# Two down projections of the last weight group, each made of seven half products instead of eight

## The chip, the core and the metric

The kernel runs on one core of one Trainium2 chip. The metric is the device time of one execution in microseconds (us), as the median of several runs. The core has a matrix engine (TensorE, PE in the profile, with PEld for its weight loads), a vector engine (VectorE, DVE), an activation engine (ScalarE, ACT), a general engine (GpSimd, POOL) and an engine that issues transfers (SyncE, SP). Each works through its own list of instructions in order and waits on semaphores for the others.

## What is computed

One transformer layer on 2048 tokens of 512 features: a gated linear attention in chunks of 128 tokens, and a feed-forward part with 4-bit weights. The change lies in the feed-forward part:

```python
vals = NVFP4_LUT[idx]                                   # two 4-bit codes per byte
W = vals.reshape(N, K // 32, 32) * scales[:, :, None]   # Wg, Wu: 4096 x 512, Wd: 512 x 4096
gate = jnp.einsum('th,nh->tn', xt, Wg)                  # xt = layernorm(x), 2048 x 512
up = jnp.einsum('th,nh->tn', xt, Wu)
inter = gelu(gate) * up
out = jnp.einsum('tn,hn->th', inter, Wd)                # the down projection
x = x + out
```

## The kernel before

Every operand of a product is split in two float16 parts, high and low, and a product is made of three matmuls (high by high, high by low, low by high) that add up in one PSUM bank. The high part is a cast on ACT, the low part a subtraction on POOL (`inter_high`, `inter_low` for the intermediates; `dequant` for the weights).

The 4096 intermediates are worked through in 8 weight groups `g` of 512. A group and a block of 512 tokens make a number `n` (`n = 4g + block`, 0 to 31). `i = 4n + j` is 128 intermediates for that token block, and a pair `m` is `i = 2m` and `2m + 1` (even and odd, `e` and `o`), so pairs `2n` and `2n + 1` are what the down projection of `n` takes. The last group has `n` 28 to 31; `n` 29 and 30 are made from pairs 58 to 61.

For a pair (m from 8 on), gate and up are each made by seven half products `P1` to `P7` of six matmuls with 256 columns (`product`), after Winograd's scheme: weights and tokens are summed beforehand, and ACT and DVE combine the results (`snapshot` on ACT copies a partial sum out of the bank, `combine` on DVE adds one to it; `C11`, `C22`, `C12` are the combined parts). The banks are few, so `P7` waits for the snapshot of `P6`, and `P4` for that of `P7`. In between, PE works at the down projection of `n = m // 2 - 1`: `down` makes one tile of 128 tokens (`tt`) from four `j` with 3 matmuls of 512 columns each, six between `P6` and `P7` (called the first place in what follows) and six between `P7` and `P4` (the second place). Down projections alternate between PSUM banks 6 and 7; DVE adds a finished tile to its rows of the output `X1` (`gather`) and frees the bank.

PE's list for one pair is thus: gate P1, P5, P2, P6, first place, P7, second place, P4, P3, then the same for up. A pair's intermediates come into the tile `fw` (gelu on ACT, times up on DVE, `inter`), the last of them (the even `i`) right after the pair's last product, when PE is already in the next pair. There, ACT makes the high parts of the pair before (`inter_high`), POOL the low parts (`inter_low`), and DVE gathers a tile of the down projection.

Weights of a group come in six chunks `k = 6g` to `6g + 5`: two for gate, two for up, two for down, each with two nibbles. Where weights must be summed (gate and up), POOL makes four sums in a chain (`dq_difference`, `dq_chain`) and then their low parts (`dq_sums`), in pairs with `m % 8` of 4 or 7. There the chain comes behind `inter_low` in POOL's list. Chunks 46 and 47, the down weights of the last group, are dequantized in pairs 56 and 57.

The order of the work is written out by hand, in a loop over `m` on each engine; semaphores count each kind of step. After pair 63 follows the down projection of `n = 31` and the last stores of `X1`.

Of the kernel before, what the change touches and what calls it, by code (L numbers as in the profile page):

```python
# [5 lines left out]
F32 = mybir.dt.float32  # L6
# [65 lines left out]

DEQUANTED = (0, 1, 4, 5, 8, 9)
# [13 lines left out]
for _i in sorted(range(NI), key=nth):  # L87
    ILO[_i] = 1 + sum(on_pool(j) == on_pool(_i) for j in ILO)
# [40 lines left out]
def block_kernel(nc, x, wqkv, bqk, bv, wab, bab, codes, scales, out, cla):  # L129
    with ExitStack() as ctx:  # L130
# [93 lines left out]

        def slot(i):
# [3 lines left out]
            return ihl_r[:, j] if n >= 3 and n % 2 else ihl_s[:, j]  # L229

# [50 lines left out]
        s_prod, s_snap, s_comb = sem("s_prod"), sem("s_snap"), sem("s_comb")  # L281
        s_half, s_done = sem("s_half"), sem("s_done")
# [17 lines left out]
        def _(eng):  # L300
# [183 lines left out]
            def products(kind, m, n, tt):  # L484
# [52 lines left out]
                down(n, tt, (0, 1))  # L537
# [25 lines left out]
            def down_last(js):  # L563
# [79 lines left out]
            banks.ring = [6, 2, 3, 7]  # L643
# [11 lines left out]
        def _(eng):  # L655
# [58 lines left out]
            def gelu(i, pg, at=0):  # L714
                if i >= 2:
# [3 lines left out]
            def inter_high(i):  # L719
                n = i // 4  # L720
                ac.wait_ge(s_inter, whole(i))
                before = {1: 0, 4: 1}[n] if n in (1, 4) else (n - 2 if n > 4 else -1)
                if before >= 0:
# [869 lines left out]
```

## Time and profile before

| | |
|---|---|
| time, median of 3 runs | 1144.14 us (1143.7 to 1144.48) |
| the profiled execution: its time, its span | 1143.82 us, 1141.8 us |
| PE busy | 1136.0 us, 99% of the span |
| DVE, POOL, ACT busy | 61%, 47%, 39% |
| chain that ended last | PE 96% |
| granted TensorE clock | 1.000 |

The span is the time from the first to the last instruction; 2.0 us of the execution lie around it. An engine's busy time is the time in which at least one of its instructions ran. Matmuls overlap: the duration shown of one (273 or 379 ns) is longer than the distance from one to the next, so the pace of PE is read from the start of one run of matmuls to the start of the next, or from the chain, whose pieces don't overlap.

### The profile page before, as it was taken

The numbers are of one execution on the slowest core, as the hardware profiler recorded it, in microseconds if no ns is written. First come the engines' busy times: TensorE is split into PE (matmuls) and PEld (weight loads), VectorE is DVE, ScalarE is ACT, GpSimd is POOL, SyncE is SP. The second block draws the span as 40 slices with busy tenths as digits, with TensorE's granted clock in tenths as the row PEclk, the third lists the DMA queues.
The fourth block names the chain that finished last, engine by engine and source line by source line (L and its number), as shares of the span: only waits on it lengthen the run. The fifth ranks groups of instructions, "written<-read, shape, count | busy, mean of one in ns | idle before, by whom it ended". The sixth has DMA issues, their size and how long they took to land.

```text
span 1141.8 us, 19963 instructions
## 1 busy us (share of the span) xinstructions
PE 1136.0 (99%) x8014; PEld 787.4 (69%) x8014; DVE 694.8 (61%) x1284; ACT 446.1 (39%) x1037; POOL 535.3 (47%) x530
## 2 busy tenths in 40 slices
PE   9999999999999999999999999999999999999999
PEld 5666655565467777777777777777777777777776
DVE  7788656367777855665566556655665566555334
ACT  4433334253344434343434343434343434343332
POOL 3386535155883945363536363635362536253110
PEclk9999999999999999999999999999999999999999
DMA  8021011000101010101010101010101010100111
GB/s 303 3 76 46 29 38 38 10 10 2 56 19 38 20 37 20 38 19 38 20 37 20 38 19 38 20 38 19 38 20 37 18 38 22 34 17 16 38 38 65
DMA packets 22828, 41.97 MB, mean 37 GB/s; under 512 B 2704, under 2 KB 3024, under 8 KB 22736
## 3 DMA queue, kind: packets, MB, share of 16 engines
q1 hardware_dynamic: 22736, 40.70, 11.3%
q8 instruction: 63, 1.03, 0.4%
q14 instruction: 29, 0.24, 0.1%
HBM read 36.46 MB, written 4.23 MB: 36 GB/s over the span
## 4 chain that ended last, share of the span: by engine, by line
PE 96%; POOL 1%; DVE 1%; ACT 0%; issue 0%; DMA 0%; SPq 0%; DVEq 0%; ACTq 0%; POOLq 0%
PE ps L518 45%; PE ps L558 29%; PE ps L348 8%; PE ps L479 7%; PE ps L314 1%; PE ps L440 1%; PE ps L423 1%; PE ps L447 1%; PE ps L434 1%; PE ps L358 1%; PE ps L414 1%; DMA WR<-wqkv 0%; POOL bigA L1302 0%; DVE wf L1122 0%; POOL kn_s L1327 0%
## 5 line engine op out<-in xcount | busy, mean ns | idle before, releaser
L558 PE MATMUL ps<-WR,ihl_s 128*128 128x512 f16 x768 | 184.7, 379 | 0.0
L518 PE MATMUL ps<-XT,WR 128*128 128x256 f16 x1344 | 183.3, 273 | 0.0
L518 PE MATMUL ps<-REG,WR 128*128 128x256 f16 x1344 | 183.3, 273 | 0.0
L1139 DVE TENSOR_TENSOR load<-load,ps 128x256 f32<-128x256 f32 x168 | 70.7, 421 | 179.8 <-PE ps L518 101.3
L558 PE MATMUL ps<-WR,vv 128*128 128x512 f16 x708 | 171.4, 379 | 0.0
L518 PEld LDWEIGHTS ps<-REG,WR 128*128 128x128 f16 x1344 | 131.5, 98 | 39.1
L814 ACT COPY load<-ps 128x256 f32<-128x256 f32 x168 | 62.6, 372 | 245.1 <-PE ps L518 245.1
L1139 DVE TENSOR_TENSOR bigB<-bigB,ps 128x256 f32<-128x256 f32 x168 | 70.6, 420 | 124.3 <-ACT bigB L814 93.2
L518 PEld LDWEIGHTS ps<-XT,WR 128*128 128x128 f16 x1344 | 131.5, 98 | 15.4
L814 ACT COPY bigB<-ps 128x256 f32<-128x256 f32 x168 | 62.6, 373 | 172.0 <-PE ps L518 172.0
L558 PEld LDWEIGHTS ps<-WR,ihl_s 128*128 128x128 f16 x768 | 75.2, 98 | 66.5
L1359 POOL TENSOR_TENSOR WR<-wf,WR 128x512 f16<-128x512 f32 x40 | 48.4, 1229 | 136.6 <-ACT WR L748 136.6
L558 PEld LDWEIGHTS ps<-WR,vv 128*128 128x128 f16 x708 | 69.3, 98 | 59.2
L1343 POOL TENSOR_TENSOR vv<-fw,vv 128x512 f16<-128x512 f32 x54 | 69.4, 1308 | 66.3 <-ACT vv L729 66.3
L1343 POOL TENSOR_TENSOR ihl_s<-fw,ihl_s 128x512 f16<-128x512 f32 x56 | 72.2, 1311 | 57.4 <-ACT ihl_s L729 57.4
L1077 DVE SCALAR_TENSOR_TENSOR X<-ps,X 128x512 f32<-128x512 f32 x127 | 86.6, 682 | 17.4 <-PE ps L558 17.3
L518 PE MATMUL ps<-REG,bigA 128*128 128x256 f16 x672 | 91.7, 273 | 0.0
L348 PE MATMUL ps<-XT,WR 128*128 128x512 f16 x384 | 86.8, 379 | 0.0
L479 PE MATMUL ps<-XT,WR 128*128 128x512 f16 x384 | 85.0, 379 | 0.0
L518 PEld LDWEIGHTS ps<-REG,bigA 128*128 128x128 f16 x672 | 65.8, 98 | 19.6 <-ACT bigB L814 0.2
L1354 POOL TENSOR_TENSOR WR<-bigC,WR 128x512 f16<-128x512 f32 x28 | 34.4, 1248 | 95.2 <-ACT WR L767 95.2
L1061 DVE SCALAR_TENSOR_TENSOR fw<-fw,bigB 128x256 f32<-128x256 f32 x112 | 72.9, 650 | 3.8
(180 smaller groups left out, 1793.6 us busy)
## 6 DMA issues: line engine op xcount, KB each, us to landing
load<-codes SPq DMA_DIRECT2D x48, 256.0 KB
load<-scales SPq DMA_DIRECT2D x48, 256.0 KB
y<-X SPq DMA_DIRECT2D x15, 256.0 KB, 2.0
bigA<-cla SPq DMA_DIRECT2D x14, 256.0 KB, 3.0
X<-x SPq DMA_DIRECT2D x3, 1024.0 KB, 13.2
WR<-wqkv SPq DMA_DIRECT2D x2, 1024.0 KB, 9.6
X<-x SPq DMA_DIRECT2D x4, 256.0 KB, 3.9
WR<-wqkv SPq DMA_DIRECT2D x4, 256.0 KB, 4.3
```

The costliest lines, as they stand in the source:

```text
L314: t = eng.transpose(PS[bank][:, 128 * kt:128 * kt + 128], src, ident[:, :])
L348: mm = eng.matmul(PS[bank][:, :], lhs, rhs, start=(n == 0), stop=(n == 11))
L479: mm = eng.matmul(bank[:, :], buf[:, wp, o + kt, 128 * j:128 * j + 128], XT[:, xp, kt, 512 * b:512 * b + 512], start=(n == 0), stop=(n == 11))
L518: mm = eng.matmul(half_bank(kind, name), w(wp, kt), x(xp, kt), start=(first and n == 0), stop=(n == 5), skip_group_check=True)
L558: mm = eng.matmul(PS[bank][:, :], ih[:, ip, 128 * tt:128 * tt + 128], buf[:, wp, 8 + j, :], start=(j == 0 and p == 0), stop=(j == end and ...
L814: eng.copy(start, half_bank(kind, name)).then_inc(s_snap, 1)
L1061: eng.scalar_tensor_tensor(w, w, GS * IS, pu, ALU.mult, ALU.mult).then_inc(s_inter, 1)
L1077: eng.scalar_tensor_tensor(X1[:, T, :], PS[bank_of["dn", n, tt]][:, :], 1.0 / (WS * IS), X1[:, T, :], ALU.mult, ALU.add).then_inc(s_ev, 1)
L1139: eng.tensor_tensor(c, c, half_bank(kind, end), ALU.add).then_inc(s_comb, 1)
L1343: eng.tensor_tensor(ih[:, 1, :], fw[:, i % 2, :], ih[:, 0, :], ALU.subtract).then_inc(s_ilop, 1)
L1354: eng.tensor_tensor(buf[:, 1, base + nib, :], wf2[:, nib, :], buf[:, 0, base + nib, :], ALU.subtract).then_inc(s_wl1, 1)
L1359: eng.tensor_tensor(buf[:, 1, base + nib, :], wf[:, nib, :], buf[:, 0, base + nib, :], ALU.subtract).then_inc(s_wlo, 1)
```

## The change

The down projections of `n` 29 and 30 (`SEVEN`) are no longer made by `down`, tile after tile. Each is a product of 512 tokens by 512 intermediates by 512 columns, and is divided in two along all three, which would make eight half products; after Winograd's scheme seven are made (`seven`), of 12 matmuls with 256 columns each. They need sums of the weights (chunks 46 and 47: the chain of four sums and their low parts, POOL in pairs 57 and 58) and of the intermediates (four differences for each of the pairs 58 to 61 on DVE, `operand_sums`, in the tile `tsum`), and high and low parts of both. The parts of a pair are now three: `e` (256 columns), `o` (512) and `T` (the four sums, 1024), by `operands_high` on ACT and `operands_low` on POOL, in place of two of 512 columns each.

The seven products take the places between gate's and up's products in pairs 60 and 61 (for `n` 29) and 62 and 63 (for `n` 30): in the even pair P1, P2, P5 and P6 in the four places, in the odd pair P3, P7 and P4, the last in two halves of six matmuls. They use banks 6 and 7 and add up there; after each, DVE adds the bank to a block of `X1` (`into_rows`), and the next product in the same bank waits for that (`s_out7`). DVE has seven such steps for an `n` where it had four.

So that the halves of the weights lie right, the host gives out the 4096 intermediates in another order, for all groups, and the rows of the down weights are read in the order `at(j)`. The stores of the rows of `n` 29 and 30 wait for `P4` and `P7`.

```diff
+SEVEN = (29, 30)
+SEVEN_PAIRS = tuple(m for n in SEVEN for m in (2 * n, 2 * n + 1))
+SUMMED = 47
+IN_TURN = ("P1", "P2", "P5", "P6", "P3", "P7", "P4")
...
+def seventh(n, name):
+
+    return 7 * (n - SEVEN[0]) + IN_TURN.index(name) + 1
+
+
+def operand(m, part):
+
+    return 3 * (m - SEVEN_PAIRS[0]) + {"e": 1, "o": 2, "T": 3}[part]
...
+        tsum = load[:, 0:2, :].bitcast(F32).rearrange("p a (t n) -> p (a t) n", t=2)
+        S1 = [two(WR0[:, a, 7, :]) for a in range(2)]
...
+        def at(j):
+
+            return 8 + 2 * (j % 2) + j // 2
...
+        def part_of(m, a, part):
+
+            first, count = {"e": (0, 1), "o": (1, 2), "T": (3, 4)}[part]
+            cols = slice(256 * (m % 2), 256 * (m % 2) + 256)
+            if m // 2 == SEVEN[0]:
+                return WR0[:, a, first:first + count, cols]
+            return ihl_s[:, 0:4, a, cols] if part == "T" else WR0[:, a, 8 + first:8 + first + count, cols]
...
+                if n in SEVEN:
+                    seven_first(kind, m, n)
+                else:
+                    down(n, tt, (0, 1))
                 pe.wait_ge(s_snap, pair_base(kind, m, 3) + 2)
                 product("P7", comb(1), sums(2))
-                down(n, tt, (3, 2))
+                if n in SEVEN:
+                    seven_second(kind, m, n)
+                else:
+                    down(n, tt, (3, 2))
...
+            def seven(n, name, tts=(0, 1)):
+
+                bank = 6 if name in ("P1", "P6", "P7", "P4") else 7
+                last = {"P1": "P4", "P2": "P3", "P5": "P2", "P3": "P5", "P6": "P1", "P7": "P6", "P4": "P7"}[name]
+                if name in ("P1", "P2"):
+                    if n > SEVEN[0]:
+                        pe.wait_ge(s_out7, seventh(n - 1, last))
+                    else:
+                        for sm, value in banks.freed[bank]:
+                            pe.wait_ge(sm, value)
+                else:
+                    pe.wait_ge(s_out7, seventh(n, last))
+                pe.wait_ge(s_whi, whi_count(SUMMED, 1))
+                pe.wait_ge(s_wlo, wlo_count(SUMMED, 1))
+                pe.wait_ge(s_wsum, pair_count(SUMMED))
+                part = {"P1": "e", "P2": "o", "P3": "o"}.get(name, "T")
+                at = {"P3": 1, "P6": 1, "P7": 2, "P4": 3}.get(name, 0)
+                pe.wait_ge(s_olo, operand(2 * n + 1, part))
...
+                for tt in tts:
+                    for u in range(2):
+                        for ip, wp in ((0, 0), (0, 1), (1, 0)):
+                            x = part_of(2 * n + u, ip, part)[:, at, 128 * tt:128 * tt + 128]
+                            mm = eng.matmul(PS[bank][:, 256 * tt:256 * tt + 256], x, weight(wp, u),
+                                            start=(name in ("P1", "P2", "P5") and tt == u == ip == wp == 0),
+                                            stop=(u == 1 and ip == 1), skip_group_check=True)
+                if tts[-1]:
+                    mm.then_inc(s_seven, 1)
...
+            def seven_first(kind, m, n):
+                if m % 2 == 0:
+                    seven(n, "P1" if kind == "gate" else "P5")
+                elif kind == "gate":
+                    seven(n, "P3")
+                else:
+                    seven(n, "P4", (0,))
+
+            def seven_second(kind, m, n):
+                if m % 2 == 0:
+                    seven(n, "P2" if kind == "gate" else "P6")
+                elif kind == "gate":
+                    seven(n, "P7")
+                else:
+                    seven(n, "P4", (1,))
...
+            def operands_high(m):
+
+                ac.wait_ge(s_inter, whole(2 * m))
+                ac.wait_ge(s_prod, pair_base("up", 55, 7) + 7)
+                if m // 2 > SEVEN[0]:
+                    ac.wait_ge(s_dn, 4 * SEVEN[0])
+                eng.copy(part_of(m, 0, "e")[:, 0, :], fw[:, 0, 0:256]).then_inc(s_ohi, 1)
+                eng.copy(part_of(m, 0, "o"), two(fw[:, 1, :])).then_inc(s_ohi, 1)
+                ac.wait_ge(s_dsum, 4 * (m - SEVEN_PAIRS[0]) + 4)
+                eng.copy(part_of(m, 0, "T"), tsum).then_inc(s_ohi, 1)
...
+                if m - 1 in SEVEN_PAIRS:
+                    operands_high(m - 1)
+                elif m > 8:
                     inter_high(oo - 2)
...
+            def into_rows(n, name):
+
+                half, odd = {"P1": (0, 0), "P2": (0, 0), "P5": (1, 1), "P6": (1, 0), "P3": (1, 0), "P7": (1, 1),
+                             "P4": (0, 1)}[name]
+                bank = 6 if name in ("P1", "P6", "P7", "P4") else 7
+                block_ = X1_of(n, half, odd)
+                dv.wait_ge(s_seven, seventh(n, name))
+                earlier = {"P2": "P1", "P3": "P6", "P7": "P5"}.get(name)
+                if earlier:
+                    dv.wait_ge(s_out7, seventh(n, earlier))
+                eng.scalar_tensor_tensor(block_, PS[bank][:, :].rearrange("p (t u n) -> p t u n", t=2, u=2),
+                                         1.0 / (WS * IS), block_, ALU.mult, ALU.add).then_inc(s_out7, 1)
+
+            def operand_sums(m):
+                e, o, at = fw[:, 0, :], fw[:, 1, :], 4 * (m - SEVEN_PAIRS[0])
+                if m > SEVEN_PAIRS[0]:
+                    dv.wait_ge(s_olo, operand(m - 1, "T"))
+                dv.wait_ge(s_inter, whole(2 * m))
+                eng.tensor_tensor(tsum[:, 0, :], e[:, 256:512], e[:, 0:256], ALU.subtract).then_inc(s_dsum, 1)
+                eng.tensor_tensor(tsum[:, 2, :], o[:, 256:512], e[:, 256:512], ALU.subtract).then_inc(s_dsum, 1)
+                dv.wait_ge(s_dsum, at + 1)
+                eng.tensor_tensor(tsum[:, 1, :], o[:, 256:512], tsum[:, 0, :], ALU.subtract).then_inc(s_dsum, 1)
+                dv.wait_ge(s_dsum, at + 3)
+                eng.tensor_tensor(tsum[:, 3, :], o[:, 0:256], tsum[:, 1, :], ALU.subtract).then_inc(s_dsum, 1)
...
+            def rows_of_second(m):
+
+                n = m // 2 - 1
+                if n in SEVEN:
+                    for name in (("P5", "P6"), ("P4",))[m % 2]:
+                        into_rows(n, name)
+                else:
+                    gather(n, 2 * m % 4 + 1)
+
...
-                    inter_low(oo - 2)
-                    inter_low(ee - 2)
-                    gather((m - 1) // 2 - 1, 2 * (m - 1) % 4 + 1)
+                    rows_of_second(m - 1)
...
-                gather(n, 2 * m % 4)
+                if n in SEVEN:
+                    for name in (("P1", "P2"), ("P3", "P7"))[m % 2]:
+                        into_rows(n, name)
+                else:
+                    gather(n, 2 * m % 4)
...
+                if m in SEVEN_PAIRS:
+                    operand_sums(m)
...
+            def operands_low(m):
+                for part, src in (("e", fw[:, 0:1, 0:256]), ("o", two(fw[:, 1, :])), ("T", tsum)):
+                    pl.wait_ge(s_ohi, operand(m, part))
+                    eng.tensor_tensor(part_of(m, 1, part), src, part_of(m, 0, part), ALU.subtract).then_inc(s_olo, 1)
...
+                if m - 1 in SEVEN_PAIRS:
+                    operands_low(m - 1)
+                elif m > 8:
                     inter_low(2 * m - 1)
                     inter_low(2 * m - 2)
+                if m == 58:
+                    dq_sums(SUMMED)
...
+                if m == 57:
+                    dq_difference(SUMMED)
+                    dq_chain(SUMMED)
...
-                sp.wait_ge(s_ev, 4 * (NI // 4 - 4) + T + 1)
+                n = NI // 4 - 4 + T // 4
+                if n in SEVEN:
+                    sp.wait_ge(s_out7, seventh(n, "P7" if T % 4 >= 2 else "P4"))
+                else:
+                    sp.wait_ge(s_ev, row_done(n, T % 4))```

POOL's list from pair 56 on, before: the low parts of chunks 46 and 47 (written to `WR`), each followed by the intermediates of a pair (to `ihl_s` or `vv`).

```order
L1343 TENSOR_TENSOR vv<-fw,vv 128x512 x2
L1359 TENSOR_TENSOR WR<-wf,WR 128x512 x2
L1343 TENSOR_TENSOR ihl_s<-fw,ihl_s 128x512 x2
L1359 TENSOR_TENSOR WR<-wf,WR 128x512 x2
L1343 TENSOR_TENSOR ihl_s<-fw,ihl_s 128x512 x2
L1343 TENSOR_TENSOR vv<-fw,vv 128x512 x4
```

The same stretch of POOL's list after the change (chunk 47 comes from `bigC` now):

```order
L1508 TENSOR_TENSOR vv<-fw,vv 128x512 x2
L1529 TENSOR_TENSOR WR<-wf,WR 128x512 x2
L1508 TENSOR_TENSOR ihl_s<-fw,ihl_s 128x512 x2
L1529 TENSOR_TENSOR WR<-bigC,WR 128x512 x2
L1536 TENSOR_TENSOR bigB<-wf 128x512
L1544 TENSOR_TENSOR wf<-wf,bigC 128x4x128
L1546 TENSOR_TENSOR wf<-wf 128x4x128
L1552 TENSOR_TENSOR bigC<-bigC,wf 128x4x128
L1508 TENSOR_TENSOR ihl_s<-fw,ihl_s 128x512 x2
L1567 TENSOR_TENSOR bigA<-bigB,bigA 128x512
L1567 TENSOR_TENSOR WR<-wf,WR 128x512
L1567 TENSOR_TENSOR bigA<-wf,bigA 128x512
```

The chain of four sums (L1536 to L1552) stands between chunk 47 and the low parts of pair 57 (the `ihl_s` row behind it).

DVE's list at the turn from pair 60 to pair 61, before: the last `inter` of pair 60, the tile gathered, and the combinations of gate of pair 61.

```order
L1061 SCALAR_TENSOR_TENSOR fw<-fw,bigB 128x512
L1077 SCALAR_TENSOR_TENSOR X1<-ps7,X1 128x512
L1139 TENSOR_TENSOR load<-load,ps4 128x256
L1139 TENSOR_TENSOR load<-load,ps3 128x256 x2
L1077 SCALAR_TENSOR_TENSOR X1<-ps6,X1 128x512
```

The same place after the change:

```order
L1188 SCALAR_TENSOR_TENSOR fw<-fw,bigB 128x512
L1225 TENSOR_TENSOR load<-fw 128x256
L1226 TENSOR_TENSOR load<-fw 128x256
L1228 TENSOR_TENSOR load<-fw,load 128x256
L1230 TENSOR_TENSOR load<-fw,load 128x256
L1217 SCALAR_TENSOR_TENSOR X1<-ps7,X1 128x4x128
L1217 SCALAR_TENSOR_TENSOR X1<-ps6,X1 128x4x128
L1291 TENSOR_TENSOR load<-load,ps4 128x256
L1291 TENSOR_TENSOR load<-load,ps3 128x256 x2
L1217 SCALAR_TENSOR_TENSOR X1<-ps7,X1 128x4x128
L1217 SCALAR_TENSOR_TENSOR X1<-ps6,X1 128x4x128
```

The four differences of intermediates stand ahead of the additions to `X1` that free banks 7 and 6.

ACT's list in the first half of a pair behind one of the pairs 58 to 61, before: the snapshot of P1, the two high parts, the snapshots of P6 and P7, and two gelus.

```order
L814 COPY load<-ps 128x256
L729 CAST vv<-fw 128x512 x2
L814 COPY load<-ps 128x256 x2
L717 ACTIVATE fw<-load 128x256
L717 ACTIVATE fw<-ps 128x256
```

The same place after the change:

```order
L933 COPY load<-ps 128x256
L843 CAST WR<-fw 128x256
L844 CAST WR<-fw 128x2x256
L846 CAST WR<-load 128x4x256
L933 COPY load<-ps 128x256 x2
L821 ACTIVATE fw<-load 128x256
L821 ACTIVATE fw<-ps 128x256
```

The high part of the sums (L846) now stands ahead of the snapshot of P6.

## Rows read from the trace of the kernel before

**Rows 1.** The page: busy times; granted clock and GB/s in 40 slices.

```profile
PE 1136.0 (99%) x8014; PEld 787.4 (69%) x8014; DVE 694.8 (61%) x1284; ACT 446.1 (39%) x1037; POOL 535.3 (47%) x530
...
PEclk9999999999999999999999999999999999999999
...
GB/s 303 3 76 46 29 38 38 10 10 2 56 19 38 20 37 20 38 19 38 20 37 20 38 19 38 20 38 19 38 20 37 18 38 22 34 17 16 38 38 65
```

**Rows 2.** The chain that ended last, from 1113 us on: start, us, what.

```profile
1113.16 3.93 PE ps L518 x36
...
1128.82 3.88 PE ps L558 x18
```

**Rows 3.** Busy time of each engine in pair 63.

```profile
1114.30:1128.65 14.35, 14.35 (x110) 10.56 (x108) 5.26 (x11) 4.60 (x11) 2.27 (x2) 1.00 0.10 38
```

**Rows 4.** Timeline, PE, pair 63: gate P1, first place, P7, second place.

```profile
1114.30 0.82 PE L518 MATMUL ps<-XT,WR 128*128 128x256 f16 x6
...
1116.92 1.46 PE L558 MATMUL ps<-WR,ihl_s 128*128 128x512 f16 x6
1118.22 0.82 PE L518 MATMUL ps<-REG,bigD 128*128 128x256 f16 x6
1118.87 1.46 PE L558 MATMUL ps<-WR,ihl_s 128*128 128x512 f16 x6
```

**Rows 5.** Timeline, DVE, pair 63: the even intermediates of pair 62, and a gather.

```profile
1114.96 0.69 DVE L1061 SCALAR_TENSOR_TENSOR fw<-fw,bigB 128x512 f32<-128x512 f32 x1
1115.57 0.68 DVE L1077 SCALAR_TENSOR_TENSOR X<-ps,X 128x512 f32<-128x512 f32 x1
```

**Rows 6.** Timeline, ACT, pair 63: snapshot of P1, high parts, snapshot of P6.

```profile
1115.21 0.37 ACT L814 COPY load<-ps 128x256 f32<-128x256 f32 x1 [2.94 <-PE ps L518]
1115.48 1.14 ACT L729 CAST vv<-fw 128x512 f16<-128x512 f32 x2
1117.12 0.37 ACT L814 COPY load<-ps 128x256 f32<-128x256 f32 x1 [0.50 <-PE ps L518]
```

**Rows 7.** Timeline, POOL, pair 63: low parts.

```profile
1116.18 2.27 POOL L1343 TENSOR_TENSOR vv<-fw,vv 128x512 f16<-128x512 f32 x2 [12.08 <-ACT vv L729]
```

**Rows 8.** Timeline around the start of pair 58: POOL twice, DVE, PE's second place.

```profile
1041.12 2.44 POOL L1359 TENSOR_TENSOR WR<-wf,WR 128x512 f16<-128x512 f32 x2 [8.31 <-ACT WR L748]
1044.43 2.27 POOL L1343 TENSOR_TENSOR ihl_s<-fw,ihl_s 128x512 f16<-128x512 f32 x2 [0.87 <-ACT ihl_s L729]
...
1043.21 0.90 DVE L1061 SCALAR_TENSOR_TENSOR fw<-fw,bigB 128x512 f32<-128x512 f32 x1
...
1047.12 1.46 PE L558 MATMUL ps<-WR,ihl_s 128*128 128x512 f16 x6
```

**Rows 9.** Timeline, POOL, pair 55: first of four chained sums, first low part behind them.

```profile
1004.07 1.27 POOL L1366 TENSOR_TENSOR bigB<-wf 128x512 f32<-128x512 f32 x1
...
1009.43 1.15 POOL L1393 TENSOR_TENSOR bigA<-bigB,bigA 128x512 f16<-128x512 f32 x1
```

**Rows 10.** Timeline, DVE (chained token sums) and POOL side by side, at 313 us.

```profile
312.91 0.68 DVE L1131 TENSOR_TENSOR REG<-REG 128x512 f32<-128x512 f32 x1
313.63 1.54 DVE L1131 TENSOR_TENSOR REG<-REG 128x512 f32<-128x512 f32 x1
...
313.46 1.16 POOL L1354 TENSOR_TENSOR WR<-bigC,WR 128x512 f16<-128x512 f32 x1 [0.63 <-ACT WR L767]
314.58 1.60 POOL L1354 TENSOR_TENSOR WR<-bigC,WR 128x512 f16<-128x512 f32 x1
```

**Rows 11.** Groups by line and form: the smallest POOL subtraction, and DVE's combinations.

```profile
L1295 POOL TENSOR_TENSOR bigD<-bigD 128x64 f16<-128x64 f32 x1 | 0.3, 315 | 0.1
L1139 DVE TENSOR_TENSOR load<-load,ps 128x256 f32<-128x256 f32 x168 | 70.7, 421 | 179.8 <-PE ps L518 101.3 <-ACT load L814 76.5
```

**Rows 12.** Timeline, PE: 19 transposes at the start, and four later on.

```profile
1.75 4.14 PE L583 MATMUL ps<-bigC 128*128 128x128 f32 x19 [1.75 <-POOL bigC L1421]
...
25.40 0.60 PE L314 MATMUL ps<-bigC,bigA 128*128 128x128 f32 x4
```

More of the change, by code:

```diff
@@ L77, in nth @@
 def nth(i):
-    return i + 1 if i < 16 else (i ^ 1) + 1
+    if i < 16:
+        return i + 1
+    return (i ^ 1) + 1 - (4 * len(SEVEN) if i // 4 > SEVEN[-1] else 0)
 def on_pool(i):
@@ L86 @@
 ILO = {}
-for _i in sorted(range(NI), key=nth):
+for _i in sorted((i for i in range(NI) if i // 4 not in SEVEN), key=nth):
     ILO[_i] = 1 + sum(on_pool(j) == on_pool(_i) for j in ILO)
@@ L188, in wide @@
                 return WRX[:, g % 2, a, j]
+            if kind == "down":
+                return WRX[:, 0, a, j]
             return GX[j][a] if g % 2 else XT[:, a, 0:2, 512 * j + 256:512 * j + 512]
@@ L544, in products, with weight @@
                 product("P3", comb(2), toks(2, 256))
+            def seven(n, name, tts=(0, 1)):
[15 more added lines that the diff above has]
+                pe.wait_ge(s_olo, operand(2 * n + 1, part))
+                def weight(wp, u):
+                    if name in ("P5", "P6", "P7", "P3"):
+                        side = {"P6": 0, "P7": 1, "P3": 2}
+                        return S1[wp][:, u, :] if name == "P5" else wide("down", 7, wp, side[name])[:, u, :]
+                    row = WR1[:, wp, (8 if name == "P1" else 10) + u, :].rearrange("p (v e n) -> p v e n", v=2, e=2)
+                    return row[:, :, 1 if name == "P4" else 0, :]
+                for tt in tts:
[7 more added lines that the diff above has]
+                    mm.then_inc(s_seven, 1)
@@ L722, in inter_high @@
                 before = {1: 0, 4: 1}[n] if n in (1, 4) else (n - 2 if n > 4 else -1)
+                if n > SEVEN[-1]:
+                    before = SEVEN[0] - 2
                 if before >= 0:
@@ L776, in dq_sums @@
                 g, base = k // 6, k % 6 // 2 * 4
-                kind = "up" if base else "gate"
+                kind = ("gate", "up", "down")[base // 4]
                 a11, a21, a12 = tiles(wf[:, :, :], 0), tiles(wf[:, :, :], 1), tiles(wf2, 0)
@@ L781, in high @@
                     return wide(kind, g, 0, j).rearrange("p k (u n) -> p k u n", u=2)
-                parts = [(flat4(tS), high(1)), (a21, tiles(WR[g % 2][:, 0, base:base + 2, :], 1)), (a11, high(0)),
-                         (a12, high(2))]
+                first_sum = flat4(WR0[:, 0, 7, :]) if k == SUMMED else tiles(WR[g % 2][:, 0, base:base + 2, :], 1)
+                parts = [(flat4(tS), high(1)), (a21, first_sum), (a11, high(0)), (a12, high(2))]
+                if k == SUMMED:
+                    ac.wait_ge(s_prod, pair_base("up", 55, 7) + 7)
                 if k == 7:
@@ L1104, in dq_finish @@
                 s, paired = place(k), k >= 6 and k % 6 < 4
-                dst = wf2 if paired and k % 2 else wf
+                dst = wf2 if paired and k % 2 or k == SUMMED else wf
                 dv.wait_ge(s_dq, 6 * k + 4)
@@ L1116, in dq_finish @@
                 for nib in range(2):
-                    if not paired and k >= 1:
+                    if not paired and k >= 1 and k != SUMMED:
                         if k >= 6 and k % 6 == 4:
@@ L1265, in _ @@
                 inter(ee, vals["up"][:, 0, :], piece(m, "even"))
-            gather(NI // 4 - 2, 3)
+                if m in SEVEN_PAIRS:
+                    operand_sums(m)
+            rows_of_second(NI // 2 - 1)
             inter_low(NI - 1)
@@ L1382, in dq_sums @@
                 g, base = k // 6, k % 6 // 2 * 4
-                kind = "up" if base else "gate"
+                kind = ("gate", "up", "down")[base // 4]
                 a11, a21, a12 = tiles(wf[:, :, :], 0), tiles(wf[:, :, :], 1), tiles(wf2, 0)
@@ L1387, in split @@
                     return [wide(kind, g, a, j).rearrange("p k (u n) -> p k u n", u=2) for a in range(2)]
-                parts = [(flat4(tS), split(1)), (a21, [tiles(WR[g % 2][:, a, base:base + 2, :], 1) for a in range(2)]),
-                         (a11, split(0)), (a12, split(2))]
+                first_sum = [flat4(WR0[:, a, 7, :]) if k == SUMMED else tiles(WR[g % 2][:, a, base:base + 2, :], 1)
+                             for a in range(2)]
+                parts = [(flat4(tS), split(1)), (a21, first_sum), (a11, split(0)), (a12, split(2))]
                 for j, (src, (hi, lo)) in enumerate(parts):
```

51 lines of the change are left out of this document (34 added, 17 removed).

## The prediction

> **What bounds the kernel now.** I read the page first: PE is busy for 99% of the span, at full granted clock in every slice [rows 1]. The chain of waits says the same for the end of the program: from 1113 us on it is matmuls, one piece after the other [rows 2]. So what PE executes counts in full, and so does any time for which it stands still. From the chain comes its pace: 36 matmuls of 256 columns take 3.93 us, 109.2 ns each; 18 of 512 columns take 3.88 us, 215.6 ns each [rows 2].
>
> Then I read one pair by engine: in pair 63 PE is busy for all of its 14.35 us, DVE for 5.26, ACT for 4.60, POOL for 2.27 [rows 3]. The others have time in all, so the question is not how much is added to them but where it stands in their lists. For that I take the timeline of pair 63 and count from its start g = 1114.30: PE is at the first place at g+2.62, at P7 at g+3.92, at the second place at g+4.57 [rows 4]; DVE ends the even intermediates of the pair before at g+1.35 and gathers until g+1.95 [rows 5]; ACT snapshots P1 at g+0.91, casts until g+2.32 and snapshots P6 from g+2.82 to g+3.19 [rows 6]; POOL's low parts take from g+1.88 to g+4.15 [rows 7]. The snapshot of P6 is thus 0.73 us early for P7, the gather 0.67 us early for the first place. These are short margins.
>
> **Part 1: the columns.** Removed are 2 x 4 tiles of 12 matmuls with 512 columns: 96 x 215.6 ns = 20.70 us. Added are 2 x 7 products of 12 with 256 columns: 168 x 109.2 ns = 18.35 us [rows 2]. PE saves 2.35 us, all of it in pairs 61 and 63, where three products stand for two tiles. Since PE has no gaps, this counts in full: -2.35 us.
>
> The Trainium skill speaks against this term: "TensorE: Matmul & The Clock Gate", section "Back-to-back issue gap", gives 131 ns as the sustained spacing at 512 columns and 81 ns at 128. An estimate from that page, halfway by columns at 256, is some 98 ns; with it the matmuls would go from 12.6 to 16.5 us, a loss of 3.9. This trace has 215.6 and 109.2 ns, proportional to columns, and the measurement decides; I give that case no chance.
>
> **Part 2: the sums of weights on POOL.** The order shows the chain of four sums behind chunk 47 and ahead of the low parts of pair 57. Those are now made from 1044.43 us on, 2.27 us for both [rows 8]; PE needs the first of them at the second place of pair 58, at 1047.12, and the second three matmuls later, at 1047.77 [rows 8]. In pair 55 the same four sums take 1009.43 - 1004.07 = 5.36 us from start to start [rows 9]. They can begin when chunk 47 ends, at 1041.12 + 2.44 = 1043.56. One thing comes on top: DVE and POOL hold each other up when both read two operands from SBUF. At 313 us a DVE subtraction takes 1.54 us instead of 0.68 while POOL works, and POOL's next one 1.60 instead of 1.16 [rows 10]. At 1043.21 DVE's `inter` is already held up (0.90 us [rows 8] against 0.69 [rows 5]) until 1044.11; the first sum then has to wait for it, 0.4 us. So the chain ends at about 1043.56 + 0.4 + 5.36 = 1049.3, the low parts of pair 57 at 1050.5 and 1051.6. PE stands from 1047.12 to 1050.5, does three matmuls, and stands again until 1051.6 and 0.05 for the semaphore: 1051.65 - 1047.77 = **+3.9 us**. Bounds: 3.4 without the collision; 4.3 with two. Behind POOL in this wait are PE's second place and ACT's gelu of pair 58, which waits for the same low parts. ACT's casts of the sums and POOL's four low parts of them follow in pair 58 as in pair 55, and are wanted only in pair 60; they cost nothing.
>
> **Part 3: the sums of intermediates, pairs 59 to 62.** Behind each of the pairs 58 to 61 DVE makes four differences of 256 columns, ahead of the addition to `X1`; ACT must wait for them before it casts `T`, and the snapshot of P6 stands behind that cast. For pairs 59 to 62 I work it out from the start of the pair:
>
> DVE: a 256-column operation takes 0.42 us [rows 11], the next may start 0.34 after it, or 0.04 after its end if it depends on it (0.68 and 313.63 - 312.91 = 0.72 in [rows 10]). Left alone, the four run 1.39, 1.73, 2.07 and 2.53 to 2.95. But POOL's low parts of `e` and `o` are due just then. ACT casts `e` from 1.38 to 1.75 and `o` until 2.3 (0.37 for 256 columns; two of 512 in 1.14 [rows 6]), and POOL starts 0.08 later (g+1.80 to g+1.88 [rows 6, 7]). [rows 10] shows what happens: operations of a dependent chain on DVE and POOL's alternate, each held up until the other's is nearly over. POOL's `e` takes about 0.68 (between 0.315 for 64 columns [rows 11] and 1.16 for 512 [rows 10]). So: two DVE differences, POOL's `e` 2.0 to 2.6, the third until 2.9, POOL's `o` 2.8 to 3.9, the fourth until 4.15.
>
> ACT: `T` has 1024 columns, 1.14 us like the two casts in [rows 6]: 4.2 to 5.3. The snapshot of P6 follows to 5.6, P7 starts at 5.65 instead of 3.92: **+1.7 us** in pairs 59 and 60.
>
> In pairs 61 and 62 another wait is longer and covers this one. The first place holds P3 (pair 61) and P1 of `n` 30 (pair 62), and both wait until DVE has added P5 or P4, from the pair before, to `X1`. That addition, 0.68 us, stands behind the four differences: 4.07 to 4.75. PE starts at 4.80 instead of 2.62: **+2.2 us** in each; P7 then comes at 6.1, after its snapshot. Pair 63 follows pair 62, which has no differences: there the addition of P5 ends at 1.95, as the gather now.
>
> Bounds of part 3: if POOL doesn't get in between, the differences end at 2.95, P7 starts at 4.45 (+0.5) and the first place at 3.60 (+1.0): 3.0 us for four pairs. If POOL gets in once (its `e` behind the third), they end at about 3.35, 0.4 later in each pair: 4.6 us. With both it is 2 x 1.7 + 2 x 2.2 = 7.8 us. I take the last, since it is the row nearest in kind, a chain of dependent DVE subtractions beside POOL's. Other additions hide: the three further `into_rows` of 0.68 lie in DVE's 9 idle us of a pair, the `T` low parts (2 us on POOL, from 5.3) are wanted in up's first place near g+11. Where P4 is halved, only six matmuls, 0.655 us, cover a snapshot that takes 0.20 + 0.37 us (P6 ends at g+2.62, its snapshot at g+3.19 [rows 4, 6]): 0 to 0.1 us, four times; I take 0.
>
> **Part 4: layout and stores.** Rows of weights are read in another order, with as many instructions. In the first place of a group chunk 6g+5 is now wanted, ready at 1043.56 for 1045.17 at the latest group; cost 0. Four stores of 0.26 MB wait until P4 of `n` 30 is added, near the end of pair 63; at the 303 GB/s of the first slice [rows 1] they take 3.5 us, and the down projection of `n` 31 starts there with 18 matmuls of 3.88 us [rows 2] and more before the next store; cost 0.
>
> **The sum.** -2.35 + 3.9 + 3.4 + 4.4 = +9.3 us. On the profiled execution's 1143.82 us that is 1153.1; the median of the runs is 0.3 above it, so I predict **1153.4 us**.
>
> **The rivals.** *DVE and POOL don't alternate* in pairs 59 to 62, or only once. For it: the second and third difference don't depend on each other, and DVE may keep its turn. Against: [rows 10]. The time is 1144.14 - 2.35 + 3.9 + 3.0 = 1148.7, or 1150.3 with one.
>
> *The clock falls.* PE stands for 3.4 us in one piece in pair 58, and the rows show no such pause at full clock. The only slow stretch is the start: 19 transposes in 4.14 us, 0.22 each, against 0.60 for four later, which is 0.11 each without the overhang of the last (a run of six at 0.109 is shown as 0.82) [rows 4, 12]. A fall that lasts as long costs 2 us: 1155.4. Against it: five shorter pauses only, and PE dense before. The skill's page on TensorE, Part 1, says that an idle array is clocked at half rate until it is busy again; no row here shows at what pause.
>
> *Only columns count*, the rival on the other side: what is late is hidden, by work that PE has in hand. It would give 1144.14 - 2.35 = 1141.8, faster by 0.2%. It needs POOL to have pair 57's second low part before 1047.77, 3.8 us sooner than worked out; the point where it decides is 1050.1 (waits below 2.35 us), and part 3 must cost nothing as well. Against it are all of parts 2 and 3.
>
> *The batch on POOL is hidden* but part 3 stands: -2.35 + 7.8 gives 1149.6. It needs the four sums to take 1.5 us; [rows 9] has 5.36.
>
> **How the numbers follow.** Forecast 0.60; no or one alternation 0.21; clock 0.12; batch hidden 0.03; only columns 0.04. The range reaches from the one-alternation case, with its low end a little under it, to the clock case with 1 us for the short places and a second collision on POOL: 1149.5 to 1156.5; the bare 1148.7, the hidden cases and anything longer stay outside. No change can be told below 0.2%, 2.3 us. Slower by more: 0.95 (all cases but one, less a little); within: 0.03; faster: 0.02.
>
> **What would show it.** In the profile after: PE idle before the down projection in pair 58, released by POOL's low part, 3.4 and 0.5 us; 96 fewer matmuls of 512 columns and 168 more of 256 at 109 ns; PE idle before P7 in pairs 59 and 60, released by ACT's snapshot, 1.7 us; before the seven-products in pairs 61 and 62, released by DVE's addition, 2.2 us; the third and fourth difference at 0.8 and 1.2 us instead of 0.42. Wrong would be: differences of 0.42 us throughout, a granted clock under 1 after 1050 us, or PE without a gap in pair 58.

## The result, and the profile after

The changed kernel takes 1157.78 us (median of 4 executions, 1156.62 to 1159.0), the kernel before beside it 1144.01. The ratio is 1.012, with a 95% interval of 1.0105 to 1.0135: 13.8 us slower. I had forecast slower, but by 9.3 us, 1153.4, and the time lies above my range of 1149.5 to 1156.5.

The profiled execution took 1156.99 us with a span of 1155.3. Its page, first the lines that answer to [rows 1], then the shares of the chain that ended last:

```profile
PE 1138.4 (99%) x8086; PEld 795.4 (69%) x8086; DVE 710.2 (61%) x1306; ACT 451.4 (39%) x1045; POOL 553.8 (48%) x542
...
PEclk9999999999999999999999999999999999999999
...
PE 93%; DVE 2%; POOL 2%; issue 1%; ACT 1%; DMA 0%; SPq 0%; DVEq 0%; POOLq 0%; ACTq 0%
```

The page alone hides what happened: PE is at 99% still, and the slices of the clock are too coarse. But PE's share of the chain fell from 96% to 93%, and other engines are in it. Who makes PE wait, with the sum, the number of times and the longest, says the view of waits of PE, from 300 us on; in the kernel before it has no row:

```profile
PE ps L624 <- DVE X L1217: 4.4, 2, 2.2
PE ps L658 <- POOL ihl_s L1508: 3.3, 1, 3.3
PE ps L560 <- ACT load L933: 2.9, 2, 1.6
```

The stretches of pairs 58 to 63, from one gate P1 to the next (the columns as in [rows 3]; before, pair 63 took 14.35 us and pairs 58 to 62 between 14.34 and 14.36; behind POOL's column stands the granted clock):

```profile
1043.32:1062.76 19.44, 16.19 (x110) 10.97 (x108) 5.48 (x11) 6.55 (x15) 13.23 (x11) 0.91 0.04 14
1062.76:1078.86 16.10, 14.53 (x110) 10.47 (x108) 8.01 (x15) 5.43 (x12) 4.23 (x3) 1.00 0.09 34
1078.86:1095.08 16.22, 14.74 (x135) 12.76 (x132) 8.70 (x16) 5.44 (x12) 4.30 (x3) 1.00 0.05 17
1095.08:1110.54 15.46, 13.27 (x122) 11.53 (x120) 9.20 (x17) 5.44 (x12) 4.30 (x3) 1.00 0.00 1
1110.54:1128.99 18.45, 16.26 (x135) 13.63 (x133) 8.70 (x16) 5.43 (x12) 4.30 (x3) 0.91 0.16 58
1128.99:1142.09 13.10, 13.10 (x123) 11.61 (x121) 6.37 (x13) 4.60 (x12) 2.28 (x2) 1.00 0.01 2
```

Against 14.35 this is +5.09, +1.75, +1.87, +1.11, +4.10 and -1.25: +12.7 us. Pair 58 begins at 1043.32 instead of 1042.55 (in [rows 8] its second place, g+4.57, is at 1047.12). Of this 0.77, 0.66 comes from the first microseconds, where the chain has the first load of weights with 4.85 us in this execution and 4.19 in that of before. Together they are the 13.5 us between the spans.

Pairs 58 and 62 stand out by their clock, 0.91. POOL (from its timeline) and PE in pair 58:

```profile
1044.29 1.73 POOL L1536 TENSOR_TENSOR bigB<-wf 128x512 f32<-128x512 f32 x1
1046.10 1.27 POOL L1544 TENSOR_TENSOR wf<-wf,bigC 128x512 f32<-128x512 f32 x1
...
1050.01 2.26 POOL L1508 TENSOR_TENSOR ihl_s<-fw,ihl_s 128x512 f16<-128x512 f32 x2
...
1047.23 0.82 PE L560 MATMUL ps<-REG,bigD 128*128 128x256 f16 x6
1051.31 2.71 PE L658 MATMUL ps<-WR,ihl_s 128*128 128x512 f16 x6 [3.25 <-POOL ihl_s L1508]
1053.81 1.29 PE L560 MATMUL ps<-REG,WR 128*128 128x256 f16 x6
```

The sums run as worked out (the first one takes 1.73 us, where the others take 1.26 or 1.27, beside a DVE operation that takes 0.91 instead of 0.69), and PE stands until the low part of pair 57. What I hadn't in the sum is the last two lines: six matmuls of 512 columns take 2.50 us from start to start instead of 1.30, and P4 is shown with 1.29 instead of 0.82. The stretches of the pause and after it, and the same for pair 62:

```profile
1047.90:1051.31 3.41, 0.16 (x3) 0.04 (x2) 0.42 (x1) 0.43 (x2) 3.33 (x4) 1.00 0.00 0
1051.31:1054.93 3.62, 3.62 (x12) 1.62 (x13) 0.00 (x0) 0.36 (x1) 0.96 (x1) 0.53 0.00 0
1054.93:1058.40 3.47, 3.47 (x33) 3.04 (x31) 1.45 (x3) 2.72 (x6) 2.30 (x3) 1.00 0.20 74
...
1111.00:1115.50 4.50, 2.33 (x22) 1.84 (x19) 4.33 (x8) 1.90 (x4) 2.17 (x2) 1.00 0.00 0
1115.52:1119.50 3.98, 3.98 (x22) 2.92 (x23) 0.41 (x2) 1.06 (x3) 2.12 (x1) 0.59 0.71 260
```

Around the end of both pauses the granted clock falls to half, the level of 1.2 GHz, stays there for some 3.4 us (0.53 and 0.59 are means over stretches that hold a little of the full clock too), and is full again. By these means the slow stretches cost (1 - 0.53) x 3.62 = 1.7 us and (1 - 0.59) x 3.98 = 1.6 us.

DVE at the turn to pair 61, with POOL and PE. Line 1228 is the third difference, 1230 the fourth, 1217 the addition to `X1`:

```profile
1096.88 0.42 DVE L1226 TENSOR_TENSOR load<-fw 128x256 f32<-128x256 f32 x1
1097.21 0.89 DVE L1228 TENSOR_TENSOR load<-fw,load 128x256 f32<-128x256 f32 x1
1098.14 1.26 DVE L1230 TENSOR_TENSOR load<-fw,load 128x256 f32<-128x256 f32 x1
1099.32 1.27 DVE L1217 SCALAR_TENSOR_TENSOR X<-ps,X 128x512 f32<-128x512 f32 x2
...
1096.94 2.17 POOL L1513 TENSOR_TENSOR WR<-fw,WR 128x256 f16<-128x256 f32 x2 [10.48 <-ACT WR L843]
...
1100.05 1.48 PE L624 MATMUL ps<-bigA,WR 128*128 128x256 f16 x12 [2.19 <-DVE X L1217]
```

The differences take turns with POOL, as forecast from [rows 10], and end 4.32 us after the pair's start at 1095.08; PE begins its first place at g+4.97 instead of g+2.62.

### The profile page after: what moved, and what is told of

The parts are those of the page before. It is cut to its first block, busy times and chain, and to the rows that moved or that the text cites. A ratio compares the mean times of both kernels' runs of the same rounds, so it can differ in the third digit from the quotient of the medians.

```text
span 1155.3 us, 20153 instructions
## 1 busy us (share of the span) xinstructions
PE 1138.4 (99%) x8086; PEld 795.4 (69%) x8086; DVE 710.2 (61%) x1306; ACT 451.4 (39%) x1045; POOL 553.8 (48%) x542
## 3 DMA queue, kind: packets, MB, share of 16 engines
HBM read 36.46 MB, written 4.23 MB: 35 GB/s over the span
## 4 chain that ended last, share of the span: by engine, by line
PE 93%; DVE 2%; POOL 2%; issue 1%; ACT 1%; DMA 0%; SPq 0%; DVEq 0%; POOLq 0%; ACTq 0%
PE ps L560 43%; PE ps L658 26%; PE ps L390 8%; PE ps L521 7%; PE ps L624 2%; PE ps L356 1%; PE ps L482 1%; PE ps L465 1%; PE ps L489 1%; PE ps L476 1%; PE ps L400 1%; PE ps L456 1%; DMA WR<-wqkv 0%; POOL WR L1529 0%; POOL bigA L1467 0%
## 5 line engine op out<-in xcount | busy, mean ns | idle before, releaser
L560 PE MATMUL ps<-REG,WR 128*128 128x256 f16 x1344 | 183.8, 273 | 0.0
L560 PE MATMUL ps<-XT,WR 128*128 128x256 f16 x1344 | 183.3, 273 | 0.0
L1291 DVE TENSOR_TENSOR load<-load,ps 128x256 f32<-128x256 f32 x168 | 70.7, 421 | 182.1 <-PE ps L560 105.4
L658 PE MATMUL ps<-WR,ihl_s 128*128 128x512 f16 x720 | 174.3, 381 | 3.3 <-POOL ihl_s L1508 3.3
L658 PE MATMUL ps<-WR,vv 128*128 128x512 f16 x660 | 159.7, 379 | 0.0
L560 PEld LDWEIGHTS ps<-REG,WR 128*128 128x128 f16 x1344 | 131.7, 98 | 38.1 <-issue 0.6
L933 ACT COPY load<-ps 128x256 f32<-128x256 f32 x168 | 62.5, 372 | 242.3 <-PE ps L560 242.3
L1291 DVE TENSOR_TENSOR bigB<-bigB,ps 128x256 f32<-128x256 f32 x168 | 70.7, 421 | 120.0 <-ACT bigB L933 91.4
L560 PEld LDWEIGHTS ps<-XT,WR 128*128 128x128 f16 x1344 | 131.5, 98 | 15.4
L933 ACT COPY bigB<-ps 128x256 f32<-128x256 f32 x168 | 62.6, 373 | 168.8 <-PE ps L560 168.8
L658 PEld LDWEIGHTS ps<-WR,ihl_s 128*128 128x128 f16 x720 | 70.6, 98 | 66.7 <-issue 4.1
L1529 POOL TENSOR_TENSOR WR<-wf,WR 128x512 f16<-128x512 f32 x38 | 46.0, 1229 | 128.3 <-ACT WR L865 128.3
L658 PEld LDWEIGHTS ps<-WR,vv 128*128 128x128 f16 x660 | 64.6, 98 | 55.3
L1204 DVE SCALAR_TENSOR_TENSOR X<-ps,X 128x512 f32<-128x512 f32 x119 | 81.2, 683 | 17.4 <-PE ps L658 17.3
L560 PE MATMUL ps<-REG,bigA 128*128 128x256 f16 x672 | 91.7, 273 | 0.0
L1508 POOL TENSOR_TENSOR vv<-fw,vv 128x512 f16<-128x512 f32 x50 | 65.0, 1322 | 42.7 <-ACT vv L835 42.7
L1508 POOL TENSOR_TENSOR ihl_s<-fw,ihl_s 128x512 f16<-128x512 f32 x52 | 67.7, 1325 | 32.2 <-ACT ihl_s L835 32.2
L560 PEld LDWEIGHTS ps<-REG,bigA 128*128 128x128 f16 x672 | 65.6, 98 | 18.8 <-ACT bigB L933 0.2
L1188 DVE SCALAR_TENSOR_TENSOR fw<-fw,bigB 128x256 f32<-128x256 f32 x112 | 73.1, 653 | 3.8
```

The lines of the kernel that those rows point to most:

```text
L560: mm = eng.matmul(half_bank(kind, name), w(wp, kt), x(xp, kt), start=(first and n == 0), stop=(n == 5), skip_group_check=True)
L933: eng.copy(start, half_bank(kind, name)).then_inc(s_snap, 1)
L1188: eng.scalar_tensor_tensor(w, w, GS * IS, pu, ALU.mult, ALU.mult).then_inc(s_inter, 1)
L1204: eng.scalar_tensor_tensor(X1[:, T, :], PS[bank_of["dn", n, tt]][:, :], 1.0 / (WS * IS), X1[:, T, :], ALU.mult, ALU.add).then_inc(s_ev, 1)
L1291: eng.tensor_tensor(c, c, half_bank(kind, end), ALU.add).then_inc(s_comb, 1)
L1508: eng.tensor_tensor(ih[:, 1, :], fw[:, i % 2, :], ih[:, 0, :], ALU.subtract).then_inc(s_ilop, 1)
```

## The experiments

Theory: the change costs what four waits cost (POOL's sums ahead of pair 57's low parts; the differences ahead of ACT's snapshot and of DVE's additions), and besides the clock falls behind pauses. The rival to the second half: the slow matmuls belong to the change, not to the pause. All times are medians; the kernel before, measured beside each, has 1144.0 to 1144.2.

**e1, the sums of weights behind pair 57's low parts.**

```diff
                 if m == 58:
+                    dq_difference(SUMMED)
+                    dq_chain(SUMMED)
                     dq_sums(SUMMED)
...
-                if m == 57:
-                    dq_difference(SUMMED)
-                    dq_chain(SUMMED)
```

> The changed kernel with one edit on POOL: the four chained sums of weights move from behind chunk 47 to behind the low parts of pair 57, as in pairs 55 and before. Theory (the batch stands in front of operands that PE needs, and the pause lets the clock fall on top): PE has no pause in pair 58, the clock doesn't fall there, and 5.1 us go (3.4 of pause, 1.7 of slow matmuls behind it): about 1152.6 from 1157.8. Rival (the slow matmuls are not from the pause): only 3.4 to 3.9 us go, about 1154, and P4 behind pair 58's second place is slow still. Pairs 59 to 62 stay as they are in both.

1152.52 us (1151.25 to 1153.55), ratio 1.0073 (1.0060 to 1.0087). 5.3 us are gone, as the theory had it, and pair 58 has no pause. The clock still falls in this profile, at the pause of pair 62 alone, though pairs 61 and 62 have pauses of the same length, 2.2 us. The rows are the pause and what follows it, for pair 61 and then for pair 62:

```profile
1092.00:1094.41 2.41, 0.23 (x4) 0.01 (x1) 2.38 (x4) 0.62 (x1) 1.47 (x2) 1.00 0.00 0
1094.41:1098.00 3.59, 3.59 (x33) 3.23 (x34) 1.29 (x3) 1.49 (x4) 2.13 (x1) 1.00 0.02 5
...
1107.40:1109.87 2.47, 0.28 (x3) 0.00 (x2) 2.44 (x4) 0.62 (x1) 1.53 (x2) 0.96 0.00 0
1109.87:1113.40 3.53, 3.53 (x18) 2.59 (x19) 0.27 (x1) 0.69 (x2) 2.12 (x1) 0.54 0.78 290
```

In pair 62 the clock is down before PE resumes (0.96 as the mean of the pause). The transfers of 290 GB/s in the last row start later, after 1110.50, so they are not what brings it down. The four executions lie at 1151.25 and 1151.65 (mean clock 0.999) and at 1153.39 and 1153.55 (0.997), which reads as one fall and two falls; only the first has a profile.

**e2, the order on DVE and ACT**, with the sums of weights left as in the change.

```diff
                     rows_of_second(m - 1)
+                if m - 1 in SEVEN_PAIRS:
+                    operand_sums(m - 1)
...
-                if m in SEVEN_PAIRS:
-                    operand_sums(m)
...
+            def sums_high(m):
+
                 ac.wait_ge(s_dsum, 4 * (m - SEVEN_PAIRS[0]) + 4)
                 eng.copy(part_of(m, 0, "T"), tsum).then_inc(s_ohi, 1)
...
                 snapshot("gate", m, "P7")
+                if m - 1 in SEVEN_PAIRS:
+                    sums_high(m - 1)
```

> The changed kernel with two edits of order: on DVE the additions to X1 go ahead of the four differences, on ACT the cast of T goes behind the snapshots of P6 and P7. Theory: all waits of pairs 59 to 62 go (1.7 + 1.7 + 2.3 + 2.3 = 8.1 us) and with them the slow matmuls in pair 62 (1.7 us); pair 58 is as before, so the time is 1144.0 - 2.35 + 5.1 = about 1146.8, plus up to 1 us of spread. Rival (the low parts of POOL or DVE's chain are late in another place, since DVE and POOL still take turns): waits of 0.5 to 1 us come back before P3 or in the first place of pairs 60 and 62, time 1148 to 1151.

1147.48 us (1145.98 to 1147.98), ratio 1.0029 (1.0018 to 1.0039). 10.3 us are gone; the forecast was about 1146.8 and up to 1 us more. Its waits of PE are those of pair 58, and 0.3 us in all, in pairs 60 and 62, for POOL's low parts:

```profile
PE ps L658 <- POOL ihl_s L1513: 3.5, 2, 3.2
PE ps L624 <- POOL WR L1518: 0.3, 2, 0.2
```

One execution had a granted clock of 1.000 and took 1145.98; the other six had 0.999 and took 1147.05 to 1147.98.

**e3, both edits together.**

> Both edits. Theory: nothing is left but the saving of columns, 96 x 215.6 - 168 x 109.2 ns = 2.35 us: 1141.7, ratio 0.998. Rival (differences of matmul columns are not what is saved, or the waits move elsewhere): 1144 or more.

1142.08 us (1141.9 to 1142.54, 11 executions), ratio 0.9983 (0.9974 to 0.9992): 1.95 us faster than the kernel before, and the granted clock is 1.0 in all of them. Of the 2.35 us of columns 0.34 goes to the two waits of 0.17 that are left, which gives 1142.0:

```profile
PE ps L624 <- POOL WR L1518: 0.3, 2, 0.2
```

**e4, e5, e5b: a pause alone.** The kernel before, with four, two or three dependent subtractions on POOL behind chunk 47 and nothing of the change.

```diff
+            def extra(count):
+
+                a, b = wf2[:, 0, :], wf2[:, 1, :]
+                for e in range(count):
+                    if e:
+                        pl.wait_ge(s_extra, e)
+                    eng.tensor_tensor(b, a, b, ALU.subtract).then_inc(s_extra, 1)
...
+                if m == 57:
+                    extra(4)
```

> The kernel before, with nothing of the change but four dependent subtractions of 512 columns on POOL behind chunk 47 (the sums are not used; no output changes). Theory (pause, then a fall of the clock because of the pause): PE pauses 3.4 us in pair 58 and matmuls behind it run at half pace for some 3 us: +5.1 us, 1149.1. Rival (my prediction's sum, no fall of the clock): +3.9 us, 1147.9.

> The kernel before with two dependent subtractions on POOL behind chunk 47 instead of four (sums not used). PE's pauses in pair 58 get 2.7 us shorter than with four: 0.7 and 0.4 us. Theory (only a long pause lets the clock fall): +1.1 us, 1145.1, granted clock 1.00 throughout. Rival (any pause costs slow matmuls behind it): +2.6 us or more.

> The same with three subtractions: a pause of 2.1 us and one of 0.4, +2.4 us without a fall of the clock, 1146.5; with one, 1.7 more, 1148.2. Theory (as long a pause as those of pairs 61 and 62 of the changed kernel brings the clock down in some executions and not in others): executions lie apart, near 1146.5 and near 1148.2. Rival (a pause of 2 us is always too short): all within 0.5 us of 1146.5.

Four: 1149.44 us, ratio 1.0046 (1.0032 to 1.0060), +5.4. Two: 1145.22, ratio 1.0009 (1.0000 to 1.0018), +1.0. Three: 1147.96, ratio 1.003 (1.002 to 1.004), +3.8. The first two are within 0.4 us of what the theory gave. The views of waits of PE, in this order:

```profile
PE ps L559 <- POOL ihl_s L1344: 3.5, 2, 3.2
```

```profile
PE ps L559 <- POOL ihl_s L1344: 0.8, 2, 0.6
```

```profile
PE ps L559 <- POOL ihl_s L1344: 2.1, 2, 1.9
```

With three the executions fall apart: 1146.30, 1146.30 and 1146.36 with a granted clock of 1.000; 1147.92, 1148.01, 1148.52, 1148.72 and 1149.06 with 0.998. The profile above is one of the first kind. With two all ten have 1.000, with four none of the four. The stretches behind the pause with four, where PE resumes at 1050.72, and P4 in them, shown with 1.49 instead of 0.82:

```profile
1050.90:1051.50 0.60, 0.60 (x3) 0.10 (x1) 0.00 (x0) 0.18 (x1) 0.60 (x1) 1.00 0.00 0
1051.50:1052.00 0.50, 0.28 (x2) 0.13 (x2) 0.00 (x0) 0.00 (x0) 0.19 (x1) 0.65 0.00 0
1052.00:1053.00 1.00, 1.00 (x3) 0.30 (x2) 0.00 (x0) 0.00 (x0) 0.00 (x0) 0.50 0.00 0
...
1053.00 1.49 PE L519 MATMUL ps<-REG,WR 128*128 128x256 f16 x6
```

In this profile pair 58 takes 19.76 us instead of 14.35, +5.4. PE resumes 3.4 us late and then 0.4 us late once more; 1.6 us are left for the clock. So the pause alone brings the slow matmuls, without the change. Between the executions with three, one fall is worth 1.6 to 2.8 us of time.

**e6, POOL's low parts behind the differences** (on top of e1).

```diff
             def operands_low(m):
+                pl.wait_ge(s_dsum, 4 * (m - SEVEN_PAIRS[0]) + 4)
```

> As e1, and POOL's low parts of a pair begin only when DVE's four differences are done, so that the two don't take turns. Theory (turns between DVE and POOL make the differences late): the third and fourth difference take 0.42 us instead of 0.9 and 1.3, the four end at g+2.95; waits of 0.4 us in pair 59 (snapshot), 1.1 in pairs 60 and 62 (now for POOL's low part of e), 1.0 in pair 61 (addition to X1), 3.7 us in all where there were 8.1, and no fall of the clock: 1144.0 - 2.35 + 3.7 = 1145.4. Rival (the differences are late for another reason, such as their length or their waits): they stay at some 4.2 us, POOL's parts come later still, and the time is 1153 or more.

1145.82 us, ratio 1.0015 (1.0005 to 1.0024), clock 1.000 in all ten. PE waits 0.3 us in pair 59, 1.1 in pairs 60 and 62 and 0.9 in pair 61, 3.4 in all where 3.7 were forecast. Left to itself DVE needs 0.42 us for each difference, here in pair 59:

```profile
1059.17 0.42 DVE L1226 TENSOR_TENSOR load<-fw 128x256 f32<-128x256 f32 x1
1059.51 0.42 DVE L1228 TENSOR_TENSOR load<-fw,load 128x256 f32<-128x256 f32 x1
1059.96 0.42 DVE L1230 TENSOR_TENSOR load<-fw,load 128x256 f32<-128x256 f32 x1
```

The taking of turns is thus what makes them late. Making one of the two wait on purpose is better than letting them collide, 1145.82 against e1's 1152.52 (which holds falls of the clock too), but worse than the order of e3.

**e7, e8: one half of e2 each** (on top of e1): DVE's additions first, or ACT's snapshots first.

> As e1, and only DVE's additions to X1 go ahead of the differences; ACT's cast of T stays ahead of the snapshot of P6. Theory (two waits share one cause, and the longer hides the shorter): the wait for the addition goes, but the differences end 0.6 to 1.2 us later, so that P7 waits in all four pairs, 2.1 to 2.6 us each: 8.4 to 10.4 us, time 1150.1 to 1152.1 plus 1.7 for each fall of the clock; no gain against e1. Rival (the addition was the cause): the waits of pairs 61 and 62 go, 1144.0 - 2.35 + 3.5 to 4.0, about 1145.5.

> As e1, and only ACT's cast of T goes behind the snapshots of P6 and P7; DVE's differences stay ahead of the additions to X1. Theory: the waits for the snapshot in pairs 59 and 60 go (1.7 each), those for the addition in pairs 61 and 62 stay at 2.3 each, 0.2 for POOL's e in pair 60: 1144.1 - 2.35 + 4.8 = 1146.6, and 1.7 more in executions in which the clock falls in the pause of pair 61 or 62. Rival (turns make the snapshot's wait come back at P4, since T is cast later): 1150.

e7: 1152.92 us, ratio 1.0078 (1.0061 to 1.0095), no better than e1. e8: 1148.68, ratio 1.0043 (1.0030 to 1.0055). The waits of PE, of e7 and then of e8:

```profile
PE ps L560 <- ACT load L933: 8.1, 4, 2.3
PE ps L624 <- POOL WR L1513: 0.3, 2, 0.2
```

```profile
PE ps L624 <- DVE X L1222: 4.4, 2, 2.2
```

In e7 the wait for the addition is gone, and that for the snapshot stands in its place, four times (2.2, 1.8, 2.3 and 1.8 us) instead of twice. One of its executions is at 1150.96 (clock 1.000), the others at 1152.66, 1153.17 and 1153.53 (0.999). They are 1.7 to 2.6 us longer, which reads as one fall each. In e8 the executions are at 1146.76 and 1146.83 (clock 1.000), 1148.39 and 1148.97 (0.999), 1150.01 and 1150.27 (0.997): no, one and two falls at the two pauses of 2.2 us, read in the same way, since the profile is of one without.

## Why the prediction was wrong, step by step

**Part 1, -2.35 us: right.** Pair 63 takes 13.10 us instead of 14.35 (-1.25); where nothing else is left (e3) the kernel is faster by the columns less two small waits. The Trainium skill, "TensorE: Matmul & The Clock Gate", section "Back-to-back issue gap", gives 131 ns at 512 columns and 81 ns at 128, by which the new matmuls would cost 3.9 us more than the old. These runs contradict it: e3 is 1.95 us faster. (The prediction's 98 ns for 256 columns lies on the straight line between the two figures, a third of the way and not halfway.)

**Part 2, +3.9 us: right in size.** PE resumed at 1051.31, and its second wait would have ended by POOL's 1050.01 + 2.26 = 1052.27 and 0.05; the undisturbed time for it is 1047.77 + 0.77 = 1048.54: 3.8 us. The view of waits doesn't show this second wait, since the three matmuls before it, at half pace, end only at some 1052.56 (an estimate: 1051.31 and half of the 2.50 us of six). In e4, at full clock there, it shows, and POOL's four subtractions alone give the same 3.8 us. (The lower bound of 3.4 should have been 3.5, 3.9 less the 0.4 of the collision.)

**Part 3, +7.8 us: right in place and cause, a little small.** Pairs 59 and 60 wait as forecast (+1.75, and 1.87 with 0.07 for its extra columns). Pairs 61 and 62 wait 2.35 us (first places at g+4.97 and g+4.98), where I had 2.18: the differences end at g+4.32, not 4.15. Sum 8.3. e6 takes away the turns of DVE and POOL, e7 the waits for the addition, e8 those for the snapshot, each by itself. The bound "without turns" is near what e6 found for pair 59.

**Part 4, 0: no term of it shows.** The stores gave no wait, and the matmuls of earlier groups have none either.

**The step that failed is the clock, which the sum had at nothing.** It stood only as the rival "the clock falls", with a chance of 0.12 and the price of one fall of 2 us, behind the pause of pair 58. In the changed kernel's profile the clock falls twice, and once behind a pause of 2.2 us, where I had no rival at all. What is left after the waits is 5.09 - 3.8 = 1.3 us in pair 58 and 4.10 - 0.07 - 2.35 = 1.7 us in pair 62. The granted clock gives the same: 1.6 us in pair 62, and 1.7 us in pair 58, of which 0.4 lies under PE's second wait. Against it I had put "five shorter pauses only, and PE dense before". e5b and e8 refute both arguments: pauses of some 2 us in a PE that is dense before and after bring the clock down in some executions. That [rows 12] show a slow stretch only at the start said nothing about pauses in the middle, since the kernel before has no pause there. The Trainium skill, "TensorE: Matmul & The Clock Gate", section "HAM oscillation", warns of long pauses of PE, behind which it is throttled again. These runs show that for 3.2 us (ten of eleven executions of e2 and e4, with a clock under 1.000) and for 1.9 us as well (five of eight of e5b).

With 3.8 + 8.3 - 2.35 the sum is +9.7; 1.3 and 1.7 for the clock make it 12.7, and 0.77 is that execution's start, 13.5 us between the spans. Waits and columns alone were forecast at +9.3 and came to +9.7; without the clock the time would have stayed in the range. The median is 0.8 us above the profiled execution: two of the four had a mean clock of 0.996 instead of 0.997 and took 1158.56 and 1159.0, which fits one more fall; those executions have no profile, so this last point is argued, not shown.

## What to carry to other kernels

Where one engine is at 99%, work added to the others costs by its place in their lists more than by its length: the same work cost 13.8 us in one order and gained 1.95 in another. Move it behind whatever the full engine waits for next, on all engines at once, since two waits that share a cause hide each other (e7). And a wait of 2 to 3 us of the matrix engine should be priced with a fall of the clock from the start: some 1.7 us a time, in 5 of 8 executions at 1.9 us and in 10 of 11 at 3.2 us.

## What was not expected of the hardware

Falls of the clock depend on the pause, but not on its length alone. With a pause of 0.6 us no execution of 10 has a mean clock under 1.000 (e5), with pauses of up to 1.1 us none of 10 (e6), with one of 1.9 us 5 of 8 (e5b), with two of 2.2 us 4 of 6 (e8), with four of 1.8 to 2.3 us 3 of 4 (e7), with one of 3.2 us 10 of 11 (e2, e4). By the times, e7's three executions have one fall each, so 3 of its 16 pauses, against 5 of 8 in e5b at nearly the same length. In e1 two pauses of 2.2 us, 15.5 us apart and with nearly the same busy times of DVE, ACT and POOL in them, had different ends in one execution.

The moment differs as well. In e1 the clock is down before PE resumes, in e4 it is full until 0.8 us after that (1050.72 to 1051.50). A row of full clock right behind a pause is thus no sign that no fall comes. What decides stays open; the runs show only that the longer pause brings a fall more often.
